# The last two batches' x multiplied with the weight first, three banks for transposes, a third unit masked by ScalarE

## What is computed

```python
# x (8, 1024, 128) f32; adj (8, 1024, 1024) int32, values 0 and 1; weight (4, 128, 128); bias (128,)
rel_ids = jnp.arange(1, 5)
masks = (adj[None] == rel_ids[:, None, None, None]).astype(x.dtype)   # only relation 1 is non-zero
h = jnp.einsum('rbnm,bmd->rbnd', masks, x)
y = jnp.einsum('rbnd,rdo->bno', h, weight) + bias
out = layernorm(x + y, axis=-1, eps=1e-5)
```

## Time and profile before

| | |
|---|---|
| median of three runs | 110.38 us (109.97 to 110.46) |
| the profiled execution | 110.12 us |
| its span, first to last instruction | 108.2 us |
| TensorE matmuls busy | 99.6 us (92%) |
| VectorE, ScalarE, GpSimd busy | 84.0, 85.4, 73.3 us |
| moved by DMA | 42.21 MB, 390 GB/s over the span |
| chain that ended last | DMA 57%, TensorE 24%, ScalarE 6%, VectorE 6% |

### The profile page before, as it was taken

The page is one execution under the profiler, slowest core; times in us unless marked ns, Lnnn a source line. Parts: engine busy times, 40 slices in busy tenths (PEclk is TensorE's granted clock), DMA queues, the critical chain, the costliest instruction groups (busy, mean ns, idle before and its releaser), DMA issues.

```text
span 108.2 us, 3036 instructions
## 1 busy us (share of the span) xinstructions
PE 99.6 (92%) x1100; PEld 92.3 (85%) x1100; DVE 84.0 (78%) x251; ACT 85.4 (79%) x103; POOL 73.3 (68%) x137
## 2 busy tenths in 40 slices
PE   5979998998999999999999999999999999999800
PEld 5947997998999999989998999899988999999700
DVE  1045879357979999798979997889888998997880
ACT  1346959969969896999699979997899788886850
POOL 3000800096089799989998999989998985923880
PEclk9999999999999999999999999999999999999995
DMA  2999999999999999999999999999999999998145
GB/s 53 359 418 415 421 416 431 436 427 404 431 430 433 407 431 418 430 427 419 428 418 425 428 427 424 424 416 434 427 418 430 424 421 424 413 424 345 47 197 197
DMA packets 7793, 42.21 MB, mean 390 GB/s; under 512 B 865, under 2 KB 994, under 8 KB 4194
## 3 DMA queue, kind: packets, MB, share of 16 engines
q1 hardware_dynamic: 7488, 40.96, 91.3%
q10 hardware_dynamic: 290, 1.05, 2.4%
HBM read 37.81 MB, written 4.19 MB: 388 GB/s over the span
## 4 chain that ended last, share of the span: by engine, by line
DMA 57%; PE 24%; ACT 6%; DVE 6%; SPq 3%; issue 1%; DVEq 0%; ACTq 0%
DMA adj_sb<-adj 57%; PE h_ps L662 11%; ACT bytes_of L525 4%; PE y_ps L674 4%; PE ids_t L640 3%; PE h_ps L714 3%; SPq L385 2%; PE ids_t L631 2%; DVE mask_t L832 1%; ACT mask_t L571 1%; DVE z_lo L817 1%; DVE stats L845 1%; DVE x_sb L895 1%; DVE moments L856 1%; ACT z_hi L563 0%
## 5 line engine op out<-in xcount | busy, mean ns | idle before, releaser
L525 ACT ACTIVATE bytes_of<-adj_sb,offset 128x2048 fp8e4<-128x2048 int32 x32 | 64.1, 2003 | 4.4 <-DMA adj_sb<-adj 3.5
L832 DVE TENSOR_SCALAR mask_t<-ids_t 128x1024 uint16<-128x1024 uint16 x62 | 40.4, 682 | 12.5 <-PE ids_t L631 11.2
L662 PE MATMUL h_ps<-mask_t,x_hi 128*128 128x256 bf16 (+1 forms) x232 | 29.2, 269 | 1.3 <-DVE mask_t L832 0.9
L662 PE MATMUL h_ps<-mask_t,x_lo 128*128 128x256 bf16 (+1 forms) x232 | 29.4, 269 | 0.2 <-DVE x_lo L900 0.2
L452 POOL TENSOR_TENSOR x_sb<-x_sb,bias_sb 128x1024 f32<-128x1024 f32 x8 | 19.0, 2380 | 10.0 <-ACT bias_sb L585 9.5
L491 POOL TENSOR_SCALAR x_sb<-x_sb,rstd,shift 128x128 f32<-128x128 f32 x55 | 23.8, 449 | 0.9
L662 PEld LDWEIGHTS h_ps<-mask_t,x_hi 128*128 128x128 f16 x232 | 21.1, 98 | 3.7 <-DVE mask_t L832 1.3
L662 PEld LDWEIGHTS h_ps<-mask_t,x_lo 128*128 128x128 f16 x232 | 21.9, 98 | 2.8 <-DVE x_lo L900 0.4
L443 POOL TENSOR_TENSOR x_lo<-x_sb,x_hi 128x1024 f16<-128x1024 f32 x6 | 12.9, 2145 | 8.2 <-ACT x_hi L538 7.8
L640 PE MATMUL ids_t<-ident,bytes_of 128*128 128x128 bf16 x192 | 16.2, 227 | 0.0
L640 PEld LDWEIGHTS ids_t<-ident,bytes_of 128*128 128x128 bf16 x192 | 14.7, 148 | 1.3 <-ACT bytes_of L525 1.0
(11 more groups left out here) (85 smaller groups left out, 84.0 us busy)
## 6 DMA issues: line engine op xcount, KB each, us to landing
adj_sb<-adj SPq DMA_DIRECT2D x28, 1024.0 KB, 24.3
adj_sb<-adj SPq DMA_DIRECT2D x8, 512.0 KB, 8.7
out<-x_sb SPq DMA_DIRECT2D x7, 512.0 KB, 21.8
x_sb<-x SPq DMA_DIRECT2D x6, 512.0 KB, 23.4
x_sb<-x ACTq DMA_DIRECT2D x2, 512.0 KB, 6.6
out<-x_sb SPq DMA_DIRECT2D x2, 256.0 KB, 2.1
w_sb<-weight SPq DMA_DIRECT2D x1, 64.0 KB, 5.9
bias_row<-bias ACTq DMA_DIRECT2D x1, 0.5 KB
```

Source lines behind the costliest of these rows:

```text
L525: nc.scalar.activation(bytes_of[:, at % ROOM].rearrange("p n t -> p t n"), adj_sb[:, slot, 2 * k:2 * k + 2, :], ACT.Square, scale=SLOPE, b ...
L662: last = nc.tensor.matmul(h_ps[g.bank][:, to], part[:, g.b % 2, j, :], mask_t[:, g.b % 2, j, cols], start=(j == 0 and part is x_hi), stop= ...
L832: nc.vector.tensor_scalar(mask_t[:, b % 2, :, u * P:(u + 1) * P].bitcast(UINT16), ids_t[bank_of(turn)][:, :, :].bitcast(UINT16), 1 << bit, ...
```

## The change

1. Batch 6 goes the way of batch 7: its x is transposed and weighed at the outset (four halves instead of two: half 0 and 1 are batch 7, 2 and 3 batch 6), and its rows are A z. Its products, copies of h and projections go. GpSimd no longer splits its x, and adds the bias to batches 6 and 7 early.
2. x of batch 6 is loaded by ACT at the outset, not by SP ahead of the adjacency of batch 6. The first two loads of SP and ACT are issued ahead of the block.
3. Three banks for transposes; the fourth bank, `other`, takes z and the rows of unit 6.
4. Unit 3 of batch 7 is masked by ScalarE too, and the lists of ScalarE, VectorE and TensorE at the end are reordered.
5. The idle turns of TensorE at the outset are 11 of 512 columns, not 44 of 128.
6. The check of the row maxima of batch 6 is taken from z, in group 5.

```diff
-    T_BANKS = 4
+    T_BANKS = 3
+    ROWS = LAST - 2
+    Z_BATCHES = (B - 1, B - 2)
...
+        def first_loads(sp, act):
+            act.dma_start(units_of(x_sb[:, 0], 0, 0, J), rows_of(x, 0, 0, J)).then_inc(s_x[0], 16)
+            sp.dma_start(adj_sb[:, 0, 0:1, :], rows_of(adj, 0, 0, 1)).then_inc(s_unit[0][0], 16)
+            act.dma_start(units_of(x_sb[:, B - 1], B - 1, 0, J), rows_of(x, B - 1, 0, J)).then_inc(s_x[B - 1], 16)
+            sp.dma_start(w_sb[:, 0, :], weight[0]).then_inc(s_w, 16)
+        first_loads(nc.sync, nc.scalar)
...
-                    if k == PAIRS - 1 and b + 1 < B - 1:
+                    if k == PAIRS - 1 and b + 1 < B - 2:
                         load_x(b + 1)
...
             act.dma_start(bias_row[:, :], ...)
+            act.dma_start(units_of(x_sb[:, B - 2], B - 2, 0, J), rows_of(x, B - 2, 0, J)).then_inc(s_x[B - 2], 16)
...
             def copy_h(g):
                 act.wait_ge(s_prod, g.index + 1)
+                if g.index == 0:
+                    act.wait_ge(s_z, 4)
...
             split_z(0)
+            split_z(1)
             check(0, 2)
-            split_z(1)
+            split_z(2)
             for g in groups[1:LAST]:
-                copy_h(groups[g.index - 1])
+                if g.index <= ROWS:
+                    copy_h(groups[g.index - 1])
...
                     if n == 0 and g.index == 1:
+                        split_z(3)
                         split_hi(1, slice(0, J), s_x[1], s_hi)
             a, a2, c, e, d = groups[LAST:]
             full, ra, rb = sets[B - 2:]
-            copy_h(groups[LAST - 1])
-            for k in (c.first // 2, e.first // 2):
-                check(a.b, k)
+            check(c.b, c.first // 2)
+            mask_second(a2.units[1])
+            root(full)
+            check(e.b, e.first // 2)
             mask_second(c.units[1])
-            root(full)
+            root(ra)
             mask_second(d.first)
-            normalise(full, full.units[4:5])
-            root(ra)
-            normalise(full, full.units[5:]).then_inc(s_aside, 1)
+            normalise(full, full.units[4:]).then_inc(s_aside, 1)
             root(rb)
...
             def project(g):
                 pe.wait_ge(s_h, g.index + 1)
                 if g.index == 0:
-                    pe.wait_ge(s_biased, 1)
+                    pe.wait_ge(s_zl, 3)
...
-            idle_turns(44, 1)
+            idle_turns(11)
...
-            transpose_last_x(0)
-            transpose_last_x(1)
-            transpose_unit(0, 2)
+            transpose_half(0)
+            transpose_half(1)
             for part in (x_hi, x_lo):
                 products(g, g.units[1:2], part)
+            transpose_unit(0, 2)
+            weigh_half(0)
+            transpose_half(2)
+            transpose_half(3)
             transpose_unit(0, 3)
-            weigh_last_x(0)
+            weigh_half(1)
             transpose_unit(0, GU)
-            weigh_last_x(1)
             products(g, g.units[2:], x_hi)
+            weigh_half(2)
             transpose_unit(0, GU + 1)
             products(g, g.units[2:], x_lo)
+            weigh_half(3)
...
-            for g in groups[1:LAST]:
+            for g in groups[1:ROWS]:
...
+            for g in groups[ROWS:LAST]:
+                n = groups[g.index + 1]
+                transpose_pair(g.b, g.units[2] // 2)
+                for u in g.units[:2]:
+                    rows_of_unit(g, u)
+                if g.index == ROWS:
+                    project(groups[g.index - 1])
+                transpose_pair(n.b, n.first // 2)
+                for u in g.units[2:]:
+                    rows_of_unit(g, u)
             a, a2, c, e, d = groups[LAST:]
             add_x(d)
             transpose_pair(a2.b, a2.first // 2)
-            project(groups[LAST - 1])
             for u in a.units:
                 rows_of_unit(a, u)
             transpose_pair(c.b, c.first // 2)
             for u in a2.units:
                 rows_of_unit(a2, u)
+            rows_of_unit(c, c.units[0])
             transpose_pair(e.b, e.first // 2)
-            for g in (c, e, d):
-                for u in g.units:
-                    rows_of_unit(g, u)
+            rows_of_unit(c, c.units[1])
+            rows_of_unit(e, e.first)
+            rows_of_unit(d, d.first)
...
             # VectorE, the end
+            sum_rows(before)
             mask_unit(a2.b, a2.units[0])
-            mask_unit(a2.b, a2.units[1])
-            sum_rows(before)
             statistics(before)
             combine(r, before, r.units)
+            sum_rows(a)
             mask_unit(c.b, c.units[0])
-            sum_rows(a)
+            offer_guess(r)
             statistics(a)
-            offer_guess(r)
+            sum_rows(a2)
             mask_unit(e.b, e.first)
-            sum_rows(a2)
             statistics(a2)
             combine(ra, a2, ra.units)
             sum_rows(c)
```

More of the change, by code:

```diff
@@ L172, in adj_resnorm_kernel @@
         x_lo = sb("x_lo", [P, 2, J, D], FP16)
-        z_hi = sb("z_hi", [P, J, D], FP16)
-        z_lo = sb("z_lo", [P, J, D], FP16)
+        z_hi = sb("z_hi", [P, 2, J, D], FP16)
+        z_lo = sb("z_lo", [P, 2, J, D], FP16)
         row_max = sb("row_max", [P, B, J], FP32)
         h_all = sb("h_all", [P, 4, GU * P], FP32)
-        x_t = h_all[:, 2:4, :]
+        x_t = [h_all[:, n, :] for n in (2, 3, 0, 1)]
         rows = x_sb
@@ L201, in adj_resnorm_kernel @@
         y_ps = pb("y_ps", [P, GU, D], FP32)
+        other = pb("other", [P, GU, D], FP32)
         spare = pb("spare", [P, GU, D], FP32)
@@ L208, in y_of, with rows_bank, z_of @@
         def y_of(g):
+            if g.index < ROWS:
+                return y_ps
             if g.index < LAST:
[L211 to L218, removed]
+                return rows_bank(g.place)
+            return (y_ps, rows_bank(0), rows_bank(1), other, spare)[g.place]
+        def rows_bank(n):
+            return h_ps[n][:, :].rearrange("p (n d) -> p n d", d=D)
         def half_of_z(half):
-            return (spare[:, :, :], h_ps[1][:, :].rearrange("p (n d) -> p n d", d=D))[half]
+            return (rows_bank(1), spare[:, :, :], y_ps[:, :, :], other[:, :, :])[half]
+        def z_of(part, half):
+            b, js = Z_BATCHES[half // 2], slice(half % 2 * HALF, (half % 2 + 1) * HALF)
+            return part[:, b - (B - 2), js]
         s_w = sem("weights_loaded")
@@ L283, in adj_resnorm_kernel, with masks_before @@
         x_v, adj_v, out_v = (t.rearrange("b (k p) d -> b p k d", p=P) for t in (x, adj, out))
+        def masks_before(u):
+            return unit_no(B - 1, 0) + min(u, 3) + len([v for v in (4, 6) if v < u])
         def wait_for_stores(engine):
@@ L496, in _ @@
             add_bias(0)
+            add_bias_late(0)
+            add_bias_late(1)
             for b in range(B - 1):
-                if b + 1 < B - 1:
+                if b + 1 < B - 2:
                     if b:
@@ L501, in _ @@
                     split_lo(b + 1)
[L502 removed]
+                    add_bias(b + 1)
                 if b >= 1:
@@ L562, in split_z @@
                 act.wait_ge(s_z, half + 1)
-                nc.scalar.activation(z_hi[:, half * HALF:(half + 1) * HALF], half_of_z(half), ACT.Copy,
+                nc.scalar.activation(z_of(z_hi, half), half_of_z(half), ACT.Copy,
                                      scale=0.5).then_inc(s_zh, 1)
             def mask_second(u):
-                act.wait_ge(s_mask, unit_no(B - 1, u) if u < J - 1 else unit_no(B - 1, u) - 1)
+                act.wait_ge(s_mask, masks_before(u))
                 act.wait_ge(s_prod, group_of(B - 3, u) + 1)
@@ L697, in rows_of_unit @@
             def rows_of_unit(g, u):
[L698 to L705, removed]
+                if u == g.first:
+                    if g.index < LAST:
+                        pe.wait_ge(s_h, g.index - 1)
+                    elif g.place < 3:
+                        pe.wait_ge(s_sum, ROWS + g.place)
+                pe.wait_ge(s_zl, 4)
+                if g.b < B - 1 or u < 3:
                     pe.wait_ge(s_mask, unit_no(g.b, u) + 1)
-                elif g.place == 3:
-                    pe.wait_ge(s_mask, unit_no(g.b, u))
+                elif u % 2 == 0:
+                    pe.wait_ge(s_mask, masks_before(u) + 1)
                 else:
-                    pe.wait_ge(s_high, 1 if g.place == 2 else 2)
+                    pe.wait_ge(s_high, (u - 1) // 2)
                 for j in range(J):
@@ L714, in rows_of_unit @@
                         last = nc.tensor.matmul(y_of(g)[:, u - g.first, :], mask_t[:, g.b % 2, j, u * P:(u + 1) * P],
-                                                part[:, j, :], start=(j == 0 and part is z_hi and g.place < 4),
+                                                part[:, g.b - (B - 2), j, :],
+                                                start=(j == 0 and part is z_hi and g.place < 4),
                                                 stop=(j == J - 1 and part is z_lo))
@@ L934, in _ @@
```

(21 more changed lines are left out.)

73 lines of the change are left out of this document (39 added, 34 removed).

## The result

The changed kernel takes 111.29 us (median of four runs, 111.01 to 111.58) against 110.38: 1.0107 times the time before, 95% interval 1.0084 to 1.0131 (the two medians alone give 1.0082). A second comparison, on another chip, gave 1.0095 (1.0074 to 1.0115). So it is slower by 0.9 to 1.2 us, more than the measurement is uncertain, and near the 111.1 forecast. The profiled execution took 111.08, its span 109.2.

A forecast was written before the change was run, and what follows sets the result against it. Loads set the pace up to batch 6, then TensorE, with hardly any slack in the middle. Transposes of (6,0) at 80.3, plus 18.6 and 4.6, put the last statistics at 103.5, 0.8 us later: 111.1 us, range 109.7 to 112.0.

The forecast's parts named there:

- 2.25 us more early work: At the outset: batch 6's transposes and weight products add 2.81 us to TensorE, less 0.56 idle won back: 2.25 us later.
- 0.78 us of slack: Middle, transposes of (2,0) to (6,0): TensorE idles only 0.78 us, so early work is absorbed only up to that.
- t0 = 80.3: Start of the transposes of pair (6,0), 78.82 before: 78.82 + 2.25 - 0.78, set by TensorE, 1.5 us later.
- the bound by the loads, 79.5: Earliest transposes of (6,0) by the loads: pair (5,3) lands at 74.2, then its check and TensorE work.
- rival A: At (6,0): TensorE wins back all, loads set t0 = 79.5; no change, 110.1 to 110.4 us; chance 0.23.
- The root ahead of the last check: End, ScalarE: the check of (7,3) waits behind batch 6's root for VectorE; its transposes start at 98.9 against 98.06.
- The list from the sum of group 11 to the variances of batch 6: VectorE's work ahead of batch 6's root: 10.4 us, ending at t0 + 16.15.
- Mask 7 behind the second root: Last unit: mask 7 waits behind the root of rows 0 to 3; 4.6 us from transposes to last statistics, at 103.5.
- What follows is unchanged: After the last statistics: combine, find, root, normalise and store stay as before, so the span is 108.2 + 0.8.
- the sum had 110.9: Whole kernel: the profiled execution's 110.12 us with +0.8 added gives 110.9.
- rival D: Outset: idle turns run at 2.4 GHz, the clock then falls, first products run slow; +2 us on top, 113; chance 0.03.

The follow-up runs named there:

- The 13 products: The kernel before with 13 extra products of 512 columns (2.81 us) on TensorE ahead of the first projection; ratio 1.0137, 1.5 us slower.
- the two without early work: The changed kernel without transposes and weight products of x of batch 6 at the outset: 1.0211 with its x loaded at the outset, 1.0033 with it loaded late.
- the kernel with the free parts only: The kernel before with three banks for transposes, 11 idle turns of 512 columns and the first loads ahead of the block; 110.09 against 110.12 us.
- two swaps on ScalarE: The changed kernel with mask 7 ahead of the second root and the check of (7,3) ahead of the root of batch 6; 110.35 us, 1.0029.

## Why the prediction was right, and where it wasn't

1. *2.25 us more early work.* Right: 18.71 + 2.25 = 20.96, measured 20.92; T(2,0) came 2.18 later. The four other profiles with this start have T(2,0) 0.3 to 0.6 later still, so the first profile is the nearest to the forecast.
2. *0.78 us of slack.* Right in kind: after shows 43.11 us from T(2,0) to T(6,0), so 0.65 of the 43.76 before came back. (Four batches at 10.75 are 43.0 us of work.) The 13 products put the whole of it, with what lies behind (6,0), at 1.2.
3. *t0 = 80.3, set by TensorE.* Measured 80.35. That it came so near is in part luck: four more profiles with the same start have 80.67, 80.71, 80.83 and 80.91. The mechanism held, as TensorE waits for no load on the way there. But the bound by the loads, 79.5, was mis-sized: it took the pair (5,3), where (5,1) decides. (5,3) does land at 47.2 + 27.1 = 74.3, as forecast; (5,1) lands at 69.3, and with 2.15 for the check and 8.5 us of work that is 80.0. TensorE was the later one by 0.4 us and not by 0.8, and rival A (t0 = 79.5, no change) had no ground.
4. *The root ahead of the last check.* The list from the sum of group 11 to the variances of batch 6 was 10.4 us; it ran from 86.02 to 96.34, 10.3. The check started at 96.57 (forecast 96.6), though its pair was ready at 93.9. The root is only the last part of that wait: turning the two alone started the check 0.67 earlier, counted from T(6,0), and the rest is mask 3, which the prediction's list for ScalarE leaves out. T(7,3) 98.70, forecast 98.9.
5. *Mask 7 behind the second root.* Statistics of d at 103.51, forecast 103.5; here two misses cancel, T(7,3) 0.2 sooner and the way from there 4.81 us and not 4.6. The idle time ahead of the last 16 products was 0.7 and not 1.1; the other 0.4 were met one unit earlier, where the products of unit 5 waited for ScalarE's mask 5, behind the late check.
6. *What follows is unchanged.* Wrong by 0.35: `found` (L970) starts 0.62 after its predecessor, 104.13 to 104.75, and 0.40 of it is "issue", where the kernel before has 0.05.

```profile
104.13 0.17 DVE wrong L967
...
104.35 0.40 issue
104.75 0.28 DVE found L970
```

The step from L967 to L970 is 0.61 to 0.62 us in all six profiles with VectorE's full new list and 0.26 to 0.27 in the eight others, the two without early work among them. The cause wasn't found. It is most of why the profiled time was 111.08 where the sum had 110.9.

7. *The clock, rival D.* The eleven turns took 4.11 us here; of the eight other profiles with them five have 4.87 or 4.88 and three 3.99 to 4.20. The 44 of 128 columns took 4.87 before and 4.06 to 4.87 in four more kernels. So both forms last alike, as taken. What D feared, slow first products, did come in one execution, of the kernel with the free parts only (below), where the slack took it. The Trainium skill, "TensorE: Matmul & The Clock Gate", section "What's actually happening", has the lower level as the state at rest; these durations agree, and the granted clock of the page, full from the first slice, doesn't show it.

## What to carry to other kernels

Work moved to the outset was free here only up to the 0.9 to 1.2 us that TensorE would have idled anyway. Two delays at a start overlapped where the added work stood ahead of the wait that the late data causes, and added up where it stood behind. A bound "by the loads" is the latest over all pairs of landing plus the work that must follow, and the pair that decides can lie well ahead of the stage looked at. In a list written out by hand, a tiny instruction that waits for another engine (a root of 0.3 us) costs all that is queued behind it: two swaps on ScalarE were worth 0.7 to 0.9 us.

## What the runs showed beyond that

TensorE's pace at the start differs between executions of nearly equal starts. In the kernel with only the free parts the first transposes and the first products took 1.05 and 1.03 us, where before they took 0.69 and 0.62:

```profile
1.19 4.88 PE L733 MATMUL h_ps<-mask_t 128*128 128x512 bf16 x11 [1.19 <-DVE mask_t L928]
6.74 1.05 PE L635 MATMUL ids_t<-ident,adj_sb 128*128 128x128 bf16 x8 [0.67 <-DMA adj_sb<-adj]
...
8.57 1.03 PE L666 MATMUL h_ps<-mask_t,x_hi 128*128 128x128 bf16 x8 [0.36 <-DVE mask_t L836]
```

It cost nothing there that the time shows, though T(2,0) moved by 1.1 us: T(6,0) came 0.3 later, the slack took the rest. A kernel without slack has to pay for any late start: in the second profile of the changed kernel the second unit's transposes waited 0.28 for their load, T(2,0) came 0.56 us later than in the first, and so did T(6,0) and the statistics of d. And a program that was only made shorter can end 1.9 us later: in two of these kernels TensorE's branch over a block of code that is not run took 3.0 and 3.1 us, where it took 0.23 to 0.47 in the others.
